# A graph network on one core: node tiles in order of edge counts, tile-by-tile transfers, four message buffers, exps by group

## What is computed

```python
h = jnp.maximum(_layernorm(x), 0.0); x = x + L0(h)  # four times, with L0 to L3
# L0: messages = x[dst] * fsum(edge_weight);  agg = segment_sum(messages, src)
#     out = softplus(agg @ Wi1 + bi1) @ Wi2 + bi2, then a batch norm with given statistics
# L1 (twice inside): h = x @ W; logit = leaky_relu(a_src[src] + a_dst[dst])
#     softmax of logit over the edges of each dst; segment_sum(h[src] * alpha, dst); layer norm
# L2: messages = relu(Wm1 [x[src], edge_attr, global]) through Wm2, mean by dst; update MLP; layer norm
# L3: as L1, with 8 heads
```

## Time and profile before

| | us |
|---|---|
| median of 3 runs | 6818.68 |
| the runs | 6813.63, 6822.79, 6818.68 |
| the profiled execution | 6817.62 |
| its span from the first to the last instruction | 6815.8 |

### The profile page before, as it was taken

One profiled execution on the slowest core, in us unless ns is written; L12 is line 12 of the kernel. 1 busy time (PEld: TensorE's weight loads), 2 busy tenths in 40 slices (PEclk: granted clock), 3 DMA queues, 4 the chain that ended last, 5 costly groups with the idle time before them and its releaser, 6 DMA issues. The chain is left out here.

```text
span 6815.8 us, 70268 instructions
## 1 busy us (share of the span) xinstructions
PE 3352.0 (49%) x17600; PEld 2903.5 (43%) x17600; DVE 3208.3 (47%) x10120; ACT 1579.2 (23%) x3899; POOL 4737.8 (70%) x4985
## 2 busy tenths in 40 slices
PE   5444300455534772555442455544477776255554
PEld 2222100455534762444432444443476664244443
DVE  8999611333322563433344433336244436465555
ACT  6000000222211761322222322223132224000000
POOL 3677777677777736777765777774777774777775
PEclk9555555666666885566656666666687777566665
DMA  2233333454544734444433444443344442444444
GB/s 72 82 119 117 119 106 101 158 172 168 172 137 144 247 122 126 150 140 146 142 102 101 150 141 145 143 130 106 104 156 148 145 146 70 127 149 144 147 146 119
DMA packets 494059, 913.17 MB, mean 134 GB/s; under 512 B 207177, under 2 KB 242336, under 8 KB 493411
## 3 DMA queue, kind: packets, MB, share of 16 engines
q1 hardware_dynamic: 343526, 617.71, 26.9%
q0 software_dynamic: 150144, 290.98, 15.5%
HBM read 663.05 MB, written 245.25 MB: 133 GB/s over the span
## 5 line engine op out<-in xcount | busy, mean ns | idle before, releaser
L1880 POOL DMA_INDIRECT edge_buf<-node_table,ixr x1472 | 1391.1, 945 | 485.2 <-issue 446.4
L1880 POOL DMA_INDIRECT Y<-node_table,ixr x1460 | 1378.0, 944 | 445.0 <-issue 445.0
L1481 DVE TENSOR_TENSOR ACC<-ACC,bank 128x129 f32 (+3 forms) x3320 | 967.5, 291 | 626.4 <-issue 117.3
L545 POOL DMA_INDIRECT edge_records<-edge_buf x782 | 753.4, 963 | 259.8 <-issue 237.6
L2152 PE MATMUL bank<-adc,turned_buf 128*128 x2199 | 298.9, 193 | 1258.5 <-DVE z L2081 764.5
L1716 POOL DMA_INDIRECT layer_messages<-edge_buf,ixr x733 | 701.9, 958 | 278.6 <-issue 223.7
L2152 PEld LDWEIGHTS bank<-adc,turned_buf 128*128 128x128 bf16 x2199 | 223.2, 102 | 1371.9 <-issue 1323.1
L1455 PE MATMUL bank<-Y 128*128 128x129 f32 (+3 forms) x2920 | 659.8, 416 | 231.7 <-DVE ACC L1481 170.4
L1455 PEld LDWEIGHTS bank<-Y 128*128 128x128 f32 x2920 | 617.2, 318 | 253.7 <-issue 245.1
L1455 PE MATMUL bank<-edge_buf,Y 128*128 128x129 f32 (+3 forms) x2944 | 625.4, 397 | 158.6 <-DVE ACC L1481 91.2
L1455 PEld LDWEIGHTS bank<-edge_buf,Y 128*128 128x128 f32 x2944 | 584.5, 300 | 176.0 <-issue 174.6
(11 more groups left out here) (387 smaller groups left out, 5750.7 us busy)
## 6 DMA issues: line engine op xcount, KB each, us to landing
Y<-onehots SPq DMA_DIRECT2D x368, 512.0 KB, 3.8
turned_buf<-onehots_turned SPq DMA_DIRECT2D x276, 256.0 KB
layer_messages<-ACC SPq DMA_DIRECT2D x28, 2112.0 KB
edge_buf<-edge_records SPq DMA_DIRECT2D x191, 288.0 KB, 3.2
onehots<-Y SPq DMA_DIRECT2D x105, 512.0 KB
XI<-layer_messages SPq DMA_DIRECT2D x84, 528.0 KB, 4.7
onehots_turned<-turned_buf SPq DMA_DIRECT2D x105, 256.0 KB
zone_oh<-onehots SPq DMA_DIRECT2D x52, 512.0 KB, 4.0
```

The costliest lines, as they stand in the source:

```text
L545: pool.indirect_dma_start(rec_d, bass.IndirectOffsetOnAxis(ap=ixs[h][:, j:j + 1], axis=0), rec[h][:, j, :], None) \
L1481: nc.vector.tensor_tensor(acc, acc, self.places.at(k, j, self.w), ALU.add).then_inc(self.added, 1)
L1880: pool.indirect_dma_start(ring[q][:, j, 0:w], None, table, bass.IndirectOffsetOnAxis(ap=ixr[q][:, j:j + 1], axis=0)).then_inc(rows_in[q], 16)
```

## The change

**Order of node tiles.** Setup ranks the 48 whole node tiles by their edge count, the smallest first; tile 48 stays last. Column block b of the on-chip arrays now holds the node tile of rank b. `node_at` (one row of 50 whole numbers in SBUF) has the first node of each block's tile. DRAM arrays indexed by node (`x`, the tables, the output) stay in the old order. So each transfer between them and a column block is now a DMA of its own, and its DRAM address comes from `node_at`: SP loads one value into a register, forms an address, and issues a DMA of 128 rows. This holds for `x` (`load_x`, 48 + 1 DMAs in place of 2), for each of the four tables (`store_rows`, 48 with a register and 1 without, in place of 13), and for the output (48 + 1 in place of 5). `load_x` waits for the ranks, and stands in the middle of SP's rounds of the scatter, after round 14.

**Buffers.** The dst pass uses `ring` with its four buffers (`DEEP`), semaphores and index tiles in place of `rows` with two.

**Exps.** `softplus_product` takes the exponentials by group, each after the next group's copy, and the logarithms and the joins in four parts of 3, 3, 3 and 4 groups.

The diff, cut to its core:

```diff
+        def node_row(engine, b):
+            return nc.values_load_multi_w_load_instructions(
+                node_at[0:1, b:b + 1], engines=[engine], min_val=0, max_val=(FULL - 1) * P,
+                skip_runtime_bounds_check_because="setup cuts them at FULL - 1")[1][0]
...
-                        sp.wait_ge(x_zero, 1)
-                        sp.dma_start(X[:, 0:FULL, :], a["x"][0:FULL * P, :].rearrange("(b p) f -> p b f", p=P)).then_inc(x_in, 16)
-                        sp.dma_start(X[0:REST, FULL, :], a["x"][FULL * P:N, :]).then_inc(x_in, 16)
+                        def load_x():
+                            sp.wait_ge(x_zero, 1)
+                            sp.wait_ge(perm_ready, 1)
+                            for b in range(FULL):
+                                sp.dma_start(X[:, b, :], a["x"][bass.ds(node_row(mybir.EngineType.SP, b), P), :]).then_inc(x_in, 16)
+                            sp.dma_start(X[0:REST, FULL, :], a["x"][FULL * P:N, :]).then_inc(x_in, 16)
...
                         for i in range(1, scatter_rounds - 1):
                             body(i, False)
+                            if i == scatter_rounds // 2:
+                                load_x()
...
+                        nc.tensor.matmul(bank[5][0:NB2, 0:1], count[0], ones[0:EP, 0:1], start=True, stop=True).then_inc(offs_in_psum, 1)
+                        pe.wait_ge(sizes_ready, 1)
+                        nc.tensor.matmul(bank[5][:, 64:64 + NB2], full_col[0:NB2, :].to_broadcast([NB2, P]), smaller[0:NB2, :],
+                                         start=True, stop=True)
...
+                        st.then(v.scalar_tensor_tensor(size_row[0:NB2, :], bank[2][0:NB2, 0:NB2], 64.0, late_row[0:NB2, :], ALU.mult, ALU.add))
+                        st.then(v.scalar_tensor_tensor(size_col[0:NB2, :], bank[5][0:NB2, 0:1], 64.0, late_col[0:NB2, :], ALU.mult, ALU.add))
...
+                        st.then(v.tensor_scalar(smaller[0:NB2, :], size_row[0:NB2, :], size_col[0:NB2, :], None, ALU.is_gt))
...
+                            if c == 3:
+                                dve.wait_ge(perm_in_psum, 1)
+                                st.then(v.tensor_scalar(node_at[:, :], bank[5][0:1, 0:NB2], float(P), None, ALU.mult))
+                                dve.sem_inc(perm_ready, 1)
...
+        def store_rows(sp, g, table, rows_out, words, stored):
+            for b in range(g * GN, min(group(g).stop, NODE_TILES)):
+                row = node_row(mybir.EngineType.SP, b) if b < FULL else FULL * P
+                sp.dma_start(table[bass.ds(row, P), :], rows_out[:, b, 0:words]).then_inc(stored, 16)
...
                         for g in range(NG):
                             sp.wait_ge(taken, g + 1)
-                            sp.dma_start(table[rows_of(g), :].rearrange("(b p) w -> p b w", p=P),
-                                         rows_out[:, group(g), 0:words]).then_inc(stored, 16)
-                        sp.wait_ge(stored, 16 * NG)
+                            store_rows(sp, g, table, rows_out, words, stored)
+                        sp.wait_ge(stored, 16 * NODE_TILES)
...
-            half_groups = (0, NG // 2, NG)
+            part_groups = (0, 3, 6, 9, NG)
...
+                        if g:
+                            exp(g - 1)
...
-                        if n >= 2:
-                            dve.wait_ge(sent[h], n // 2 * (16 * G))
-                        nc.vector.tensor_copy(rows[h][:, :, D:D + 1], fields[:, t:t + G, R_SLOC - EA:R_SLOC - EA + 1]) \
+                        if n >= DEEP:
+                            dve.wait_ge(sent[r], n // DEEP * (16 * G))
+                        nc.vector.tensor_copy(ring[r][:, :, D:D + 1], fields[:, t:t + G, R_SLOC - EA:R_SLOC - EA + 1]) \
...
                         sp.wait_ge(part_ready[n], 1)
-                        sp.dma_start(out[tiles.start * P:whole * P, :].rearrange("(b p) f -> p b f", p=P),
-                                     X[:, tiles.start:whole, :]).then_inc(written, 16)
+                        for b in range(tiles.start, min(tiles.stop, FULL)):
+                            sp.dma_start(out[bass.ds(node_row(mybir.EngineType.SP, b), P), :], X[:, b, :]).then_inc(written, 16)
```

More of the change, by code:

```diff
@@ L613, in _ @@
                         pe.wait_ge(upto_ready, 1)
-                        for q in range(3):
+                        for q in range(5):
                             nc.tensor.transpose(bank[q % 2][0:NB2, q // 2 * P:q // 2 * P + P], upto[q], ident[:, :]) \
@@ L1285, in softplus_product @@
                                  "prod", "taken", "steps"))
-            half_groups = (0, NG // 2, NG)
-            half = [slice(half_groups[n] * words, min(half_groups[n + 1] * words, NBP * P)) for n in range(2)]
+            part_groups = (0, 3, 6, 9, NG)
+            parts = [slice(part_groups[n] * words, min(part_groups[n + 1] * words, NBP * P)) for n in range(4)]
             with nc.Block() as block:
@@ L1304, in _ @@
                     dve.wait_ge(z_out, NG)
-                    for n in range(2):
+                    for n in range(4):
                         dve.wait_ge(logs, n + 1)
-                        v.scalar_tensor_tensor(flat[0][:, half[n]], flat[0][:, half[n]], 0.0, flat[1][:, half[n]],
+                        v.scalar_tensor_tensor(flat[0][:, parts[n]], flat[0][:, parts[n]], 0.0, flat[1][:, parts[n]],
                                                ALU.max, ALU.add).then_inc(halves, 1)
-                    dve.wait_ge(halves, 2)
+                    dve.wait_ge(halves, 4)
                     for g in range(NG):
@@ L1332, in _ @@
                     for g in range(NG):
-                        pe.wait_ge(halves, 1 if g < half_groups[1] else 2)
+                        pe.wait_ge(halves, sum(at <= g for at in part_groups))
                         if g >= 2:
@@ L1349, in copy, with exp @@
                         nc.scalar.copy(part_of(stT[g % 2], g), part_of(bank[g % 2], g)).then_inc(turned_sb, 1)
+                    def exp(g):
+                        act.wait_ge(absolute, g + 1)
+                        nc.scalar.activation(flat[1][:, rows_of(g)], flat[1][:, rows_of(g)], ACT.Exp, bias=zero1[:, :], scale=-1.0) \
+                            .then_inc(exps, 1)
                     copy(0)
@@ L1358, in _ @@
                                              bias=bias[:, 0:1]).then_inc(absolute, 1)
-                    act.wait_ge(absolute, NG)
-                    for n in range(2):
-                        nc.scalar.activation(flat[1][:, half[n]], flat[1][:, half[n]], ACT.Exp, bias=zero1[:, :], scale=-1.0) \
-                            .then_inc(exps, 1)
-                    for n in range(2):
-                        act.wait_ge(exps, n + 1)
-                        nc.scalar.activation(flat[1][:, half[n]], flat[1][:, half[n]], ACT.Ln, bias=one1[:, :]).then_inc(logs, 1)
+                    exp(NG - 1)
+                    for n in range(4):
+                        act.wait_ge(exps, part_groups[n + 1])
+                        nc.scalar.activation(flat[1][:, parts[n]], flat[1][:, parts[n]], ACT.Ln, bias=one1[:, :]).then_inc(logs, 1)
         one1 = sb("one1", [P, 1])
@@ L1620, in scale_zone @@
                             .then_inc(zone_scaled, 1)
-                    for h in range(2):
-                        nc.vector.memset(rows[h][:, :, D:D + 8], 0.0).then_inc(cleared, 1)
+                    for r in range(DEEP):
+                        nc.vector.memset(ring[r][:, :, D:D + 8], 0.0).then_inc(cleared, 1)
                     nc.vector.memset(one1[:, :], 1.0)
@@ L1724, in _ @@
                                                         acc_rows[:, j, 0:MW], None).then_inc(zone_sent, 16)
-                    for h in range(2):
-                        pool.wait_ge(sent[h], 16 * sum(tiles_in(n) for n in range(h, REG_HALVES, 2)))
+                    for r in range(DEEP):
+                        pool.wait_ge(sent[r], 16 * sum(tiles_in(n) for n in range(r, REG_HALVES, DEEP)))
                     pool.wait_ge(zone_sent, 16 * ZT)
```

173 lines of the change are left out of this document (116 added, 57 removed).

## The result

| | us |
|---|---|
| before, median of 4 runs | 6817.98 |
| after, median of 4 runs (6901.77 to 6905.86) | 6903.03 |
| ratio after / before, 95% interval | 1.0126 (1.0111 to 1.0141) |
| predicted | 6883.0 (6857 to 7015) |

The changed kernel is 85 us slower, 1.26%, and the interval of the ratio lies clear of 1. The measured time lies 20 us above the forecast and inside its range; sign and places came out as forecast. The profiled execution of after took 6902.04 us, with a span of 6900.3.

A forecast was written before the change was run, and what follows sets the result against it. POOL bounds scatters and gathers at 1.26 us a tile; SP's transfers decide the stages between. 41.5 + 21.6 + 14.7 + 4.5 - 14.5 - 2.4 = +65.4 on the profiled 6817.6 gives 6883 us, range 6857 to 7015.

The forecast's parts named there:

- The rest of a tile: SP's list for one table tile: register load 0.157, address step 0.046, DMA 0.36, gaps of 0.04; 0.69 us in all.
- The table stores: Four table stages: SP needs 48 x 0.69 = 33.1 us in each, so the last stores start later, +41.5 us.
- The output: Final output: bound by SP from its first tile, 48 x 0.70 = 33.6 us, last DMA later by +21.6.
- The load of x: Setup: 48 x 0.76 = 36.5 us of x on SP delays round 15's attributes, POOL stands still, +14.7 us.
- Ranks: Setup ahead of the first slot round: 19 more DVE steps of 0.238 us delay POOL's first scatter, +4.5 us.
- PE's wait: Setup: PE waits for DVE's sizes with filter sums queued behind; costed at nothing, up to 5 us if cover fails.
- Four buffers: Dst pass: 43 POOL waits for DVE's scaling, 27.4 us less 12.9 of POOL's own step, go: -14.5 us.
- Exps by group: Softplus: exponentials inside the loop give back about 0.8 us, a smaller last join 1.6; -2.4, between -8.7 and +1.5.
- The case forecast: Whole kernel: the forecast of 6883 us, with the buffers' -14.5 or without; chance 0.60.
- The flat load: Rival on SP's register loads: one to eight values cost the same 0.597 us; +192.0, 7010 us; chance 0.31.
- SP not bound: Rival: load and address step go on beside DMA issue, 0.40 to 0.43 us a tile; -3.8, 6814 us; chance 0.06.
- buffers without effect: Rival on the dst pass: DVE's own zone-half work held POOL, so -14.5 is gone, 6898 us; within the forecast's 0.60.

## Why the prediction was right, and where it was short

- **SP bounds the stages with transfers by register: right.** The four table stages span the same 39 us, whatever they had, and taking loads or tiles off SP shortens them by as much as it should: 10 us a stage with loads by four, 19.4 in the output with two queues. What SP costs when there is no register address to form, 19 us of 90, shows that the registers and not the number of transfers are the main part.
- **The rest of a tile.** MOVE and the gaps, of which I had counted one too few, are 0.05 more; the DMA was 0.03 cheaper (0.332 for 0.36) and the address step 0.01. The worry that a DMA with a register address takes longer than 0.36 was not borne out: it is quicker than one directly behind another. All in all 0.806 for 0.69.
- **The table stores: mechanism right, size off.** The same sum with 0.806 gives 48 x 0.806 = 38.7, and +18.0, +10.1, +19.0, +16.8 for the four: 63.9, where the stages show 65.3. With 0.69 it was 41.5. This is more than the whole of the miss of 19.6. The other terms are off by 6.3 upwards and, with the rest of the kernel, by 11.0 downwards; that they take back 5 us is luck.
- **The output.** 48 x 0.806 = 38.7 puts the last DMA 26.7 us later in the stage; it is 27.4 (39.4 us behind SP's start for 12.0). But the stage ends 3.6 us after the start of that DMA in place of 6.4: before, a DMA of 768 KB was issued 0.4 us ahead of it, now one of 64 KB. The prediction had left that out. Of the 5.8 us by which the DMA is later than forecast 2.8 are given back, so that +24.7 stands for +21.6.
- **The load of x.** One long stall at 736 behind round 14, ended by late attributes, as forecast; 17.3 us for 14.7, mostly from the 39.7 us for 48 tiles in place of 36.5 (here the DMA was put at 0.43 and took 0.333, which hid part of the load's error). Spreading the tiles removes it.
- **Ranks.** The first slot round starts 4.8 us later than in the earlier trace rows for the 4.5 forecast (the row of after is below), and POOL's first scatter is 4.8 later (199.1 for 194.3). PE's wait was hidden, as put.

```profile
79.82 0.44 DVE L879 TENSOR_SCALAR Y<-Y,iota_row 128x168 bf16<-128x168 bf16 x2
```

- **Four buffers: right kind, too small.** -19.4 for -14.5. I summed only the waits that the profile gives to DVE, and took 43 of them with 0.30 off each. Of these 14.5 only 10.4 went. "Issue" held 13.7 us more that were not POOL's own step, and 11.6 of them went too; the start and the end of the pass took 2 us more. The earlier trace rows and the view that gave the 54.8 had it: 223.7 us in 689 places is 0.325 each, not 0.30. "The rest of the stage is POOL's own 1.26 us a tile" was wrong by that.
- **Exps by group: too small.** -6.2 for -2.4. The step that failed is "1.9 us a group in place of 1.51", on both sides. I added durations and left out that ACT starts an instruction before the last one has ended: it is 1.66. And 1.51 was every other group; with the 1.72 between them the mean is 1.61. So the groups give back some 0.5 us, not 4.7: ACT used time in which it had waited for DVE. The table load and the last group took more than put, some 2.5 us for 1.6, so the loop saved 4.0 where 0.8 was forecast. The finer parts gave 2.2 for 1.6.
- **The chances.** The case forecast, SP bound and the buffers with effect, came true, at a price of the load between the two bounds. The flat load, at 0.31, is refuted by the 0.270; SP not bound by the 39 us; buffers without effect by the run with them alone.

Put together: the tables are 23.8 us above the forecast, the output 3.1 and setup 3.2; the small edits are 4.9 and 3.8 below it, and the rest of the kernel 2.3. That is +19.1, of the 19.6 us by which the sum of 65.4 fell short of 85.0.

## What to carry to other kernels

Where an address comes from a register, price the whole list of the issuing engine for one transfer, and compare it with the pace at which the data comes; here 0.81 us a tile against 0.43 to 0.6. Load addresses by four from a column that is a multiple of four, and spread the transfers over queues of idle engines: that took back 75 of 90 us. A pace is read from several rounds, not from one pair: it can alternate. An idle stretch marked "issue" is an engine's own only up to its usual length; the rest of it is a wait without a name and may go with the same edit. A reordering that no stage profits from, as here, costs its transfers and nothing pays for them.

## What was not expected of the hardware

- Register loads on SP from SBUF: 0.27, 0.49, 0.69 us for 1, 2, 3 values, 0.30 for 4, 0.53 for 8, 0.755 for 12, 0.98 for 16 from a start that is a multiple of four, and 1.28 for 6 values from one that is not (0.76 from one that is).
- The DMA of a whole tile takes SP 0.432 us directly behind another, and 0.32 to 0.33 behind a wait or the steps of a register address.
- POOL issues a plain store of one tile in 0.54 us (median of 48), less than the 0.95 of an indirect one.
- In setup's scatter POOL stops for 1.8 us after every 112 scatters (at 346.2, 489.3 and 632.3 us of after; 341.7, 484.7 and 627.7 of before), marked "issue". In the dst pass with two buffers such stops go on, five of them again 112 scatters apart and up to 3.7 us long; with four, one of 1.85 us is left, and with three one of 2.04. In the gathers no stretch marked "issue" is over 0.45 us. What they are is open.
